# Cross attention with hard memory picks and a routed FFN: transposed projection, row-tiled heads, a router folded into the output projection, and routing per group

## The chip, the core and the metric

The kernel runs on one core of one Trainium2 chip. The metric is the device time of one execution in microseconds; three runs of the kernel before took 468.86, 470.2 and 472.27 us. All engines of the core have instruction streams of their own: PE (TensorE), DVE (VectorE), ACT (ScalarE), POOL (GpSimd) and SP (SyncE, which only issues DMAs here). They meet at semaphores, and every stream works in the order in which it is written.

## What is computed

The input `x` is (2, 1024, 256), that is 16 tiles of 128 tokens; the context has 77 rows per batch.

```python
def _L0_xattn_ref(q, kv, Wq, Wkv, Wc):
    qp = jnp.einsum('bld,ed->ble', q, Wq)
    scores = jnp.einsum('bld,bmd->blm', qp, kv)
    idx = jnp.argmax(scores, axis=-1)                     # one of 77 context rows per token
    mem = jnp.take_along_axis(kv, idx[..., None], axis=1)
    mkv = jnp.einsum('bld,ed->ble', mem, Wkv)
    mk, mv = jnp.split(mkv, 2, axis=-1)                   # 16 wide, shared by the 16 heads
    qh = qp.reshape(b, l, h, dh).transpose(0, 2, 1, 3)
    logits = jnp.einsum('bhld,bmd->bhlm', qh, mk) * scale
    attn = jax.nn.softmax(logits, axis=-1)
    out = jnp.einsum('bhlm,bmd->bhld', attn, mv)
    return jnp.einsum('bld,ed->ble', out, Wc)             # after merging the heads

x = x + xattn(layernorm(x), ctx, Wq, Wkv, Wc)
# FFN: 8 experts, 2 per token, gate = silu; hidden 256, inner 512, twice
x = x + ffn(layernorm(x), w1, w2, router_w)
```

The memory rows of a batch are copies of at most 77 different rows, so both kernels attend over the 77 context rows, each weighted by how often it was picked, and leave out those that were never picked.

## The kernel before

The program has four parts. **The head** (lines 328 to 337 on SP) loads `x`, the small weights and 12 MB of expert weights (`raw`, 8 DMAs), normalises the tokens of one batch after the other, takes the scores against the 77 rows (L943), picks the largest (`picks`) and counts the picks (`counts`, `masks`). **The attention** then goes over NH = 4 groups of 512 tokens. In a loop over u from -1 to 4, each with 10 slots, the queries of group u+1 are prepared while group u is attended and group u-1 is finished. To prepare is: normalise again (`normalise`, L678), transpose (`prep_x`, L965), project (`prep_project`, L972), lay each head out in 64 columns as high part, low part, a one and the high part again (`qs`, L509 and L684), transpose those (`prep_turn`, L985), and multiply with the keys `bd` to have the maxima (`prep_logits`, L998, `maxima`, L693). To attend is: per pair of heads two products of 77 x 512 with the keys and two that subtract the maxima (`logits`, L1017 and L1019, into the banks 0 and 1), the exponential (`exps`, L488), and per four heads the sums with the values in four column tiles of the array (`sums`, L1032), which are turned back (L1039) and divided (L777, L779). To finish (`post`) is: transpose (L1045), output projection (L1064), residual (L703), the second layernorm (L707 to L719, `pow` on POOL in L428), transpose again (L1045), router product (L1078), and the top two experts by maxima and comparisons on DVE (L737 to L761).

Beside this ACT splits the expert weights: `high(n)` (L477 to L481) writes chunk n of 48, rounded, into `W`, which overlies `raw` two chunks off; POOL subtracts it from the raw chunk (L411) into one of two buffers `low`; and `high(n + 2)` on ACT waits for that, issues its DMA to DRAM (`lows`, L477) and overwrites the raw chunk.

**The routing** comes once all groups are done (L1119 to L1130, L841 to L879): counts per expert, the slot of each token, one-hot tables, a list `idx` of rows per block. SP brings the low parts back (`W1lo` in L362 once the attention has used `qT`, `W2lo` in L369 over `X` once the last layernorm has read it) and the last rows (L351) behind them. **The FFN loop** (L1141 to L1178) works off 39 blocks of 128 rows, each gathered by an indirect DMA (L448), and starts when index, low parts and rows are there. The change does not touch it.

## Time and profile before

| | |
|---|---|
| runs | 468.86, 470.2, 472.27 us (median 470.2) |
| span of the profiled execution | 468.0 us; its own time is not among the runs, the median is 2.2 us above its span |
| PE busy | 376.7 us (80%) |
| DVE busy | 221.9 us (47%) |
| ACT busy | 197.3 us (42%) |
| POOL busy | 171.6 us (37%) |
| head, then groups 0, 1, 2 | to 67.8, 106.5, 145.8 and 184 us |
| group 3, finish of group 3, routing | to 208, 230 and 251.3 us |
| FFN loop | 251.3 to 468 us |

The ends of the groups are the starts of the first L1017 of each group; the others are read from the timeline. The span runs from the first to the last instruction. A busy share is an average over these parts, so each part is read for itself. In the rows, an arrow `<-` behind idle time names what ended it, and the granted TensorE clock is given as a share of 2.4 GHz.

### The profile page before, as it was taken

How to read it: one execution, taken by the hardware profiler on the slowest of the kernel's cores; microseconds unless marked ns; L12 is line 12 of the kernel's file. 1: busy time of each engine (PE TensorE's matmuls, PEld its weight loads, DVE VectorE, ACT ScalarE, POOL GpSimd, SP SyncE). 2: the span in 40 equal slices, each digit the busy share in tenths (PEclk: the TensorE clock that was granted, in tenths of full speed). 3: DMA queues.
4: the chain of work that ended last, by engine and by line, in shares of the span. 5: the costliest groups of instructions: out<-in, count | busy, mean ns of one | idle time of the engine just before them, and what ended most of it. 6: DMA issues, size and time to landing. Idle time of an engine off the chain costs nothing.

```text
span 468.0 us, 7576 instructions
## 1 busy us (share of the span) xinstructions
PE 376.7 (80%) x2262; PEld 282.8 (60%) x2263; DVE 221.9 (47%) x535; ACT 197.3 (42%) x376; POOL 171.6 (37%) x148
## 2 busy tenths in 40 slices
PE   1758688879999988765514999999999999999980
PEld 1647565558677655343513677777777777677760
DVE  4576734545674764543382344344344344343430
ACT  0324546666657664420101444444444444344330
POOL 2021633433333353320003245545545545544521
PEclk9967979999979998876555999999999999999986
DMA  8999110111212112229611032332332332332320
GB/s 266 386 387 336 57 34 34 46 45 35 69 45 82 68 57 87 73 91 349 223 48 46 8 62 47 57 57 46 55 59 46 51 63 46 47 67 46 50 32 11
DMA packets 35317, 43.44 MB, mean 93 GB/s; under 512 B 3200, under 2 KB 27904, under 8 KB 35296
## 3 DMA queue, kind: packets, MB, share of 16 engines
q1 hardware_dynamic: 20896, 26.49, 16.5%
q0 software_dynamic: 7488, 10.39, 13.6%
q10 hardware_dynamic: 6912, 6.29, 4.0%
q8 instruction: 12, 0.20, 0.2%
q14 instruction: 9, 0.07, 0.0%
HBM read 27.23 MB, written 15.93 MB: 92 GB/s over the span
## 4 chain that ended last, share of the span: by engine, by line
PE 74%; DVE 12%; ACT 4%; issue 4%; DMA 2%; POOL 1%; SPq 1%; DVEq 0%; POOLq 0%; ACTq 0%
PE ps L1155 24%; PE ps L1166 12%; PE ps L1173 4%; PE ps L985 4%; PE ps L972 4%; PE ps L1064 3%; PE ps L998 3%; PE ps L1017 3%; PE ps L1019 3%; PE ps L1032 3%; PE ps L1045 2%; PE ps L1141 2%; PE ps L1078 2%; ACT qs L509 1%; PE ps L943 1%
## 5 line engine op out<-in xcount | busy, mean ns | idle before, releaser
L445 POOL DMA_INDIRECT out_x<-oT,idx x39 | 61.8, 1586 | 98.8 <-ACT oT L558 98.8
L411 POOL TENSOR_TENSOR low<-raw,W 128x512 bf16 (+1 forms) x48 | 62.0, 1295 | 95.4 <-DMA lows<-low 79.6
L1155 PE MATMUL ps<-W,qs 128*128 x312 | 83.6, 411 | 1.2 <-DVE qs L884 1.2
L1155 PEld LDWEIGHTS ps<-W,qs 128*128 128x128 f32 x312 | 57.4, 191 | 13.2 <-issue 1.6
L890 DVE TENSOR_TENSOR uT<-uT,ps 128x512 f32<-128x512 f32 x39 | 26.8, 687 | 69.9 <-ACT uT L564 69.9
L564 ACT ACTIVATE uT<-ps 128x512 f32<-128x512 f32 x39 | 23.4, 599 | 85.9 <-PE ps L1155 85.9
L448 POOL DMA_INDIRECT xr<-rows,idx x39 | 38.7, 991 | 38.5 <-DVE idx L874 26.9
L894 DVE TENSOR_TENSOR qs<-ps,mT 128x512 fp32r<-128x512 f32 x39 | 27.0, 692 | 49.3 <-ACT mT L570 49.3
L1155 PE MATMUL ps<-W1lo,xpT 128*128 x156 | 41.3, 388 | 0.0
L693 DVE TENSOR_REDUCE mx<-ps 128x8 f32<-128x616 f32 x32 | 25.5, 798 | 32.7 <-PE ps L998 32.6
L488 ACT ACTIVATE pT<-ps 77x1024 f32<-77x1024 f32 x32 | 32.7, 1022 | 13.7 <-PE ps L1019 13.7
L985 PE MATMUL ps<-ident,qs 128*128 128x128 f32 x128 | 21.9, 297 | 13.5 <-DVE qs L684 8.8
L1166 PE MATMUL ps<-W,mT 128*128 x156 | 28.7, 307 | 2.0 <-DVE xpT L895 2.0
L481 ACT CAST W<-raw 128x512 fp32r<-128x512 f32 x48 | 29.8, 621 | 0.2
L1017 PE MATMUL ps<-qT,bd 128*77 128x512 f32 x64 | 29.3, 458 | 0.5 <-ACT pT L488 0.3
L558 ACT ACTIVATE oT<-ps,xr 128x256 f32<-128x256 f32 x39 | 18.5, 474 | 24.2 <-PE ps L1166 23.3
L1173 PE MATMUL ps<-ident,uT 128*128 128x128 f32 x156 | 24.3, 278 | 5.0 <-issue 3.9
L985 PEld LDWEIGHTS ps<-ident,qs 128*128 128x128 f32 x128 | 15.5, 151 | 19.6 <-DVE qs L684 16.8
L1019 PE MATMUL ps<-mT,neg 128*77 128x512 f32 x64 | 26.1, 408 | 0.0
L1166 PE MATMUL ps<-W,qs 128*128 x156 | 25.3, 285 | 0.0
L998 PEld LDWEIGHTS ps<-bd,qT 128*128 128x128 f32 x128 | 19.9, 203 | 8.6 <-issue 4.2
L494 ACT CAST qT<-ps 128x512 fp32r<-128x512 f32 x32 | 18.8, 587 | 14.4 <-PE ps L985 14.3
(171 smaller groups left out, 641.9 us busy)
## 6 DMA issues: line engine op xcount, KB each, us to landing
raw<-in_w SPq DMA_DIRECT2D x8, 1536.0 KB, 17.0
lows<-low ACTq DMA_DIRECT2D x48, 128.0 KB, 1.7
W1lo<-lows SPq DMA_DIRECT2D x8, 512.0 KB, 7.7
rows<-xr SPq DMA_DIRECT2D x4, 528.0 KB, 3.3
X<-in_x SPq DMA_DIRECT2D x2, 1024.0 KB, 6.9
out_x<-X SPq DMA_DIRECT2D x4, 512.0 KB, 3.3
X<-lows SPq DMA_DIRECT2D x8, 256.0 KB, 4.4
xr<-rows,idx POOLq DMA_INDIRECT x39, 2.8
```

Source lines behind the costliest of these rows:

```text
L411: pool.tensor_tensor(low[:, j, :], was, high.bitcast(F32), ALU.subtract).then_inc(low_ok, 1)
L445: pool.indirect_dma_start(out=out, out_offset=at_rows(c), in_=ob[:, c % GR, :], in_offset=None, compute_op=ALU.add).then_inc(sc_out, 16)
L448: pool.indirect_dma_start(out=xg[:, b % GR, :], out_offset=None, in_=rows, in_offset=at_rows(b)).then_inc(g_in[b % GR], 16)
L481: act.copy(W[:, n, :], raw[:, n + 2, :]).then_inc(hi_ok, 1)
L488: act.activation(pT[0:NK, 2 * (n % 4):2 * (n % 4) + 2, :], ps[0:NK, 0:2, :], ACT.Exp).then_inc(ex_ok, 1)
L985: mm = pe.transpose(ps[:, 5, n * P:(n + 1) * P], qs[:, a:a + 2, :].rearrange("p h w -> p (h w)"), ident[:])
L998: mm = pe.matmul(ps[:, 6 + n // 2, (n % 2) * 2 * NK:(n % 2 + 1) * 2 * NK], qT[:, w % 2, 4 * g + n, t * P:(t + 1) * P], bd[:, w // 2, :], s ...
L1017: pe.matmul(ps[0:NK, o, :], bd[:, u // 2, o * NK:(o + 1) * NK], qT[:, u % 2, p, :], start=True, stop=False)
L1019: mm = pe.matmul(ps[0:NK, o, :], neg[:, 2 * p + o:2 * p + o + 1].broadcast_to([P, NK]), mT[:], start=False, stop=True)
L1155: mm = pe.matmul(ps[:, f, :], part[:, c * P:(c + 1) * P], chunk(wts, e * per + (2 * c + f)), start=(k == 0 and c == 0), stop=(k == 2 and c ...
L1166: mm = pe.matmul(ps[:, 4, 0:D], part[:, c * P:(c + 1) * P], w2, start=(k == 0 and c == 0), stop=(k == 2 and c == FC - 1))
L1173: mm = pe.transpose(ps[:, 3, c * P:(c + 1) * P], yb[:, c * P:(c + 1) * P], ident[:])
```

## The change

- **Head.** `x` comes in four DMAs. The small weights are issued by ACT. POOL normalises (one `tensor_scalar` per tile, behind its `pow`). The 8 router columns, with the mean taken out, stand beside the 77 score columns in `GT`, so one product of 85 columns gives scores and the router's share of `x`. DVE picks with `max` and `max_index`.
- **Transposed projection.** `project` multiplies the weights, as the stationary operand, with the transposed tokens, 512 at a time, so the queries arrive transposed: `qh` and `ql`, high and low part, for all four groups before the attention starts. `prep_turn`, its copies and the second layernorm of the queries go.
- **Row-tiled heads.** `logits` multiplies in two row tiles of 64 rows, 308 columns each, three times (high with high, low with high, high with low), per tile and half of the heads. `scores_turned` takes four heads at a time: 16 products of 32 rows and 512 columns in four row tiles, into the banks 0 to 3. One exponential covers 2048 columns. `uT` is copied by ACT instead of DVE.
- **Router in the output projection.** `WC` gets 8 columns more, the product of output projection and router (once, L1103). The second transpose and the router product go; `residual` works per tile of 128 tokens and adds the share of `x`; the top two come from `max` and `max_index`.
- **Routing per group.** `ranks`, `places` and `table` work off group v beside the attention of group v+2; at the end the last two groups' share, the totals and one product that selects the blocks remain.
- **Low parts.** SP issues their DMAs, in one stream with the raw weights, the residuals and the rows; the number of `high` calls per slot stands in a table.

```diff
+STEPS = 4
+SLOTS = 2 * STEPS
+COUNTS = (6, 5)
+HIGH_HEAD = (0, 2, 3, 3)
+HIGH_SLOT = (2, 1, 1, 1, 2, 1, 1, 1)
+HIGH_FIRST = sum(HIGH_HEAD)
+def high_before(u, k):
+    n = HIGH_FIRST + u * sum(HIGH_SLOT) + sum(HIGH_SLOT[:k])
+    return min(NC, n)
...
+            def keep_lows(start, stop):
+                for n in range(start, stop):
+                    sp.wait_ge(low_ok, n + 1)
+                    sp.dma_start(lows[n], low[:, n % LR, :]).then_inc(low_out[n % LR], 16)
...
+            kept = 0
+            for v in range(NH - 1):
+                at = high_before(v + 1, SLOTS - 1)
+                keep_lows(kept, at)
                 keep_residual(v)
+                kept = high_before(v + 2, 2)
+                keep_lows(at, kept)
                 keep_rows(v)
...
+            for u in range(NH):
+                here = slice(u * HT, (u + 1) * HT)
+                pool.wait_ge(ln_v, u + 1)
+                pool.tensor_tensor(rs[:, here], ve[:, here], half[:], ALU.pow).then_inc(ln_r, 1)
+                pool.wait_ge(ln_r, u + 1)
+                for i in range(HT):
+                    q = u * HT + i
+                    if u:
+                        pool.wait_ge(x_tr, 2 * (u - 1) + i // 2 + 1)
+                    pool.tensor_scalar(xn[:, i, :], X[:, q, :], mv[:, q, 0:1], rs[:, q:q + 1],
+                                       ALU.subtract, ALU.mult).then_inc(xn_ok, 1)
...
-            def high(n):
-                if 2 <= n < NC + 2:
-                    act.wait_ge(low_ok, n - 1)
-                    act.dma_start(lows[n - 2], low[:, n % 2, :]).then_inc(low_out[n % 2], 16)
-                if n < NC:
...
+            def high(count):
+                for _ in range(count):
+                    n = highs[0]
+                    if n >= NC:
+                        return
+                    highs[0] += 1
+                    if n >= 2:
+                        act.wait_ge(low_ok, n - 1)
                     if n % EC == 0:
                         act.wait_ge(raw_in[n // EC], 16)
                     act.copy(W[:, n, :], raw[:, n + 2, :]).then_inc(hi_ok, 1)
...
+                q_high(u, 0)
+                q_high(u, 1)
+                high(HIGH_HEAD[u])
...
+            def residual(v, i):
+                q = v * HT + i
+                dve.wait_ge(wc_mm, q + 1)
+                dve.tensor_tensor(X[:, q, :], X[:, q, :], ps[:, 5, 0:D], ALU.add).then_inc(x2_ok, 1)
+                dve.tensor_tensor(g2[:, i, :], ps[:, 5, D:RW], x0[:, q, :], ALU.add).then_inc(g2_ok, 1)
+                dve.wait_ge(x2_ok, q + 1)
+                dve.bn_stats(st2[:, i, :], X[:, q, :]).then_inc(st2_ok, 1)
+                dve.wait_ge(g2_ok, q + 1)
+                dve.max(v8[:, i, :], g2[:, i, :]).then_inc(top, 1)
+                dve.wait_ge(st2_ok, q + 1)
+                dve.bn_aggr(mv2[:, i, :], st2[:, i, :]).then_inc(mv2_ok, 1)
+                dve.wait_ge(top, TOPS * v + 2 * i + 1)
+                dve.max_index(j8[:, i, :], v8[:, i, :], g2[:, i, :]).then_inc(top, 1)
...
+            def choose(v):
+                dve.wait_ge(mv2_ok, (v + 1) * HT)
+                dve.tensor_scalar(rs2[:], mv2[:, :, 1], EPS, None, ALU.add).then_inc(v2_ok, 1)
+                dve.wait_ge(top, TOPS * v + 2 * HT)
+                dve.tensor_copy(ef[:], j8[:, :, 0:2].rearrange("p t k -> p k t")).then_inc(top, 1)
+                dve.wait_ge(top, TOPS * v + 2 * HT + 1)
+                dve.tensor_tensor(o12[:].rearrange("p k t e -> p (k t) e"),
+                                  iota_f[:, 0:E].unsqueeze(1).broadcast_to([P, 2 * HT, E]),
+                                  ef[:].rearrange("p k t -> p (k t)").unsqueeze(2).broadcast_to([P, 2 * HT, E]),
+                                  ALU.is_equal).then_inc(top, 1)
...
+                dve.wait_ge(pre_mm, v + 1)
+                rank = ps[:, 5, 320:320 + HT * E].rearrange("p (t e) -> p t e", e=E)
+                for k in range(2):
+                    dve.tensor_tensor(pr[:, k], o12[:, k], rank, ALU.mult).then_inc(sl_ok, 1)
+                dve.wait_ge(sl_ok, 2 * v + 2)
+                link(dve.tensor_reduce(slot[:], pr[:].rearrange("p k t e -> p (k t) e"), AX.X, ALU.add))
+                link(dve.tensor_copy(sloti[:], slot[:]))
+                link(dve.tensor_scalar(rmi[:], sloti[:], P - 1, None, ALU.bitwise_and))
...
+                for n in range(2 * HT):
+                    i = n % HT
+                    dve.tensor_scalar(bval[:, n, :], iota_h[:], colf[:, n:n + 1], tok_f[:, v * HT + i:v * HT + i + 1],
+                                      ALU.is_equal, ALU.mult).then_inc(hot_ok, 1)
+                    dve.tensor_scalar(asel[:, n, :], iota_h[:], rmf[:, n:n + 1], None, ALU.is_equal).then_inc(hot_ok, 1)
...
-                for n in range(4):
-                    a = 2 * (4 * g + n)
-                    mm = pe.transpose(ps[:, 5, n * P:(n + 1) * P], qs[:, a:a + 2, :].rearrange("p h w -> p (h w)"),
-                                      ident[:])
-                mm.then_inc(q_tr, 1)
...
-                for n in range(4):
-                    mm = pe.matmul(ps[:, 6 + n // 2, (n % 2) * 2 * NK:(n % 2 + 1) * 2 * NK],
-                                   qT[:, w % 2, 4 * g + n, t * P:(t + 1) * P], bd[:, w // 2, :], start=True, stop=True)
-                mm.then_inc(l1_mm, 1)
...
-                for o in range(2):
-                    pe.matmul(ps[0:NK, o, :], bd[:, u // 2, o * NK:(o + 1) * NK], qT[:, u % 2, p, :],
-                              start=True, stop=False)
-                    mm = pe.matmul(ps[0:NK, o, :], neg[:, 2 * p + o:2 * p + o + 1].broadcast_to([P, NK]), mT[:],
-                                   start=False, stop=True)
-                mm.then_inc(l2_mm, 1)
...
-                if k == 5:
-                    pe.wait_ge(xn2_ok, (v + 1) * HT)
-                    turn(xn2, 0, x2_tr)
-                if k == 6:
-                    pe.wait_ge(x2T_ok, 2 * v + 1)
-                    turn(xn2, 1, x2_tr)
-                if k == 7:
-                    pe.wait_ge(x2T_ok, 2 * v + 2)
-                    for i in range(HT):
-                        for c in range(DC):
-                            mm = pe.matmul(ps[:, 3, i * E:(i + 1) * E], oT[:, i, c, :], RT[:, c, :],
-                                           start=(c == 0), stop=(c == DC - 1))
-                    mm.then_inc(r_mm, 1)
...
+            def project(u, j):
+                if u == 0:
+                    pe.wait_ge(wqt_in, 16)
+                else:
+                    pe.wait_ge(ql_ok, 2 * (u - 1) + j + 1)
+                for c in range(DC):
+                    mm = pe.matmul(ps[:, 4 + j, :], WQT[:, c, j * P:(j + 1) * P], xT[:, u % 2, c, :],
+                                   start=(c == 0), stop=(c == DC - 1))
+                mm.then_inc(q_mm, 1)
...
+                    pe.wait_ge(mx_ok, u * SLOTS + k)
+                for n, (part, hl) in enumerate(((qh, 0), (ql, 0), (qh, 1))):
+                    for r in range(2):
+                        half_ = slice(r * 64, (r + 1) * 64)
+                        mm = pe.matmul(ps[:, 6 + r, 0:HT * NK], part[half_, u, j, t * P:(t + 1) * P],
+                                       kb[half_, u // 2, hl].rearrange("p h n -> p (h n)"), start=(n == 0), stop=(n == 2))
+                mm.then_inc(l1_mm, 1)
...
+                    pe.wait_ge(xT_ok, 2 * NH)
+                    pe.wait_ge(sc_used, NH)
+                else:
+                    pe.wait_ge(ex_ok, n)
+                for m, (part, hl) in enumerate(((qh, 0), (ql, 0), (qh, 1), (None, 0))):
+                    for r in range(4):
+                        quad = slice(r * 32, (r + 1) * 32)
+                        if part is not None:
+                            keys, rhs = kb[quad, u // 2, hl, (2 * r + o) % 4, :], part[quad, u, j, :]
+                        else:
+                            h = j * 8 + 2 * r + o
+                            keys, rhs = sel[quad, h:h + 1].broadcast_to([32, NK]), mT[quad, :]
+                        mm = pe.matmul(ps[0:NK, r, :], keys, rhs, start=(m == 0), stop=(m == 3))
+                mm.then_inc(l2_mm, 1)
...
+                if i:
+                    pe.wait_ge(x2_ok, v * HT + i)
+                    pe.wait_ge(g2_ok, v * HT + i)
+                for c in range(DC):
+                    mm = pe.matmul(ps[:, 5, 0:RW], oT[:, i, c, :], WC[:, c, :], start=(c == 0), stop=(c == DC - 1))
+                mm.then_inc(wc_mm, 1)
...
+            for u in range(NH + 1):
+                for k in range(SLOTS):
+                    if u < NH and k % 2 == 0:
+                        scores_turned(u, k // 2)
+                    if u + 1 < NH:
+                        logits(u + 1, k)
+                    if u < NH and k % 2 == 1:
+                        sums(u, k // 2)
+                    if u >= 1 and k in (1, 2):
+                        turn_heads(u - 1, k - 1)
+                    if u < NH and k % 2 == 0 and k:
+                        turn_sums(u, k // 2 - 1)
+                    if u >= 1 and k == 0:
+                        turn_sums(u - 1, STEPS - 1)
+                    if u == 0 and k == 2:
+                        counts(1)
+                    if u >= 1 and 3 <= k <= 6:
+                        combine(u - 1, k - 3)
+                    if u >= 2 and k == 0:
+                        ranks(u - 2)
+                    if u >= 2 and k == 7:
+                        place(u - 2)
+                if u + 1 < NH:
```

**The order on SP.** The SP queue before, between the raw weights and the group loop:

```order
L335 DMA X<-in_x 128x8x256
L337 DMA raw<-in_w 128x6x512 x8
L341 DMA rows<-xr 128x264
L342 DMA out_x<-xr 128x256
L354 UNCONDITIONAL_BRANCH
```

and in the change, where the 48 DMAs of `low` stand in this queue:

```order
L303 DMA X<-in_x 128x4x256 x4
L306 DMA raw<-in_w 128x6x512 x8
L310 DMA rows<-xr 128x264
L311 DMA out_x<-xr 128x256
L316 DMA lows<-low 128x512 x27
L320 DMA out_x<-X 128x4x256
L316 DMA lows<-low 128x512 x4
L325 DMA rows<-xr 128x4x264
```

The low parts were issued by ACT before; now they are behind the raw weights and the two padding rows (L310, L311), and between them SP waits for a group's residual and rows.

**The order on ACT in the head of the change** (`pT` here is `xT`, `qhl` the high parts of the queries, `W` the rounded weights):

```order
L457 CAST W<-raw 128x512 [waits raw_in0]
L457 CAST W<-raw 128x512
L462 COPY pT<-ps 128x2x2x128 [waits x_tr] x2
L467 CAST qhl<-ps 128x512 [waits q_mm] x2
L457 CAST W<-raw 128x512 [waits low_ok] x3
L462 COPY pT<-ps 128x2x2x128 [waits x_tr] x2
L467 CAST qhl<-ps 128x512 [waits q_mm] x2
L457 CAST W<-raw 128x512 [waits low_ok]
```

Three casts of weights (chunks 2, 3 and 4) stand between the queries of the third and the fourth group.

**The order on PE in the attention.** Before, one slot of 10 of a group:

```order
L985 MATMUL ps<-ident,qs 128x128 [waits qT_ok,q_lo]
L985 MATMUL ps<-ident,qs 128x128 x3
L1017 MATMUL ps<-qT,bd 77x512 [waits ex_ok]
L1019 MATMUL ps<-mT,neg 77x512
L1017 MATMUL ps<-qT,bd 77x512
L1019 MATMUL ps<-mT,neg 77x512
L998 MATMUL ps<-bd,qT 128x154 [waits mx_ok,qT_ok]
L998 MATMUL ps<-bd,qT 128x154 x3
```

and in the change two slots of 8 of a group (L1013 is `scores_turned`, L974 `logits`, L1032 `turn_sums`, L1059 `combine`, L1024 `sums`):

```order
L1013 MATMUL ps<-qhl,kb 77x512 [waits ex_ok]
L1013 MATMUL ps<-qhl,kb 77x512 x11
L1013 MATMUL ps<-mT,sel 77x512 x4
L974 MATMUL ps<-kb,qhl 128x308 [waits mx_ok,ql_ok]
L974 MATMUL ps<-kb,qhl 128x308 x5
L1032 MATMUL ps<-ident,uT 128x128 [waits ut_ok]
L1032 MATMUL ps<-ident,uT 128x128 x3
L1059 MATMUL ps<-WC,oT 128x264 [waits g2_ok,x2_ok,oT_ok]
L1059 MATMUL ps<-WC,oT 128x264
L974 MATMUL ps<-kb,qhl 128x308 [waits mx_ok,ql_ok]
L974 MATMUL ps<-kb,qhl 128x308 x5
L1024 MATMUL ps<-pT,vc 32x512 [waits on_ok,ex_ok]
```

The transposes and the projection are out of the group; a product of four heads takes the place of two products of two heads.

## Rows read from the trace of the kernel before

**Rows 1.** Busy time per stretch: start:end, length, then engines, clock, DMA.

```profile
0.00:67.80 67.80, 42.48 (x257) 36.47 (x259) 40.02 (x125) 22.87 (x44) 18.35 (x28) 0.85 0.72 253
67.80:106.50 38.70, 31.90 (x204) 22.28 (x203) 17.22 (x32) 26.33 (x43) 14.81 (x12) 1.00 0.12 39
106.50:145.80 39.30, 36.43 (x229) 28.05 (x228) 24.86 (x62) 24.83 (x43) 14.44 (x12) 0.91 0.18 62
145.80:184.00 38.20, 32.81 (x201) 22.81 (x200) 22.55 (x55) 23.13 (x37) 15.03 (x12) 0.96 0.21 70
184.00:208.00 24.00, 18.16 (x102) 11.34 (x100) 14.31 (x44) 8.97 (x13) 7.42 (x7) 0.86 0.17 56
208.00:230.00 22.00, 14.43 (x44) 10.68 (x44) 4.89 (x16) 1.82 (x4) 1.01 (x1) 0.58 0.93 295
230.00:251.30 21.30, 3.32 (x64) 2.77 (x64) 16.33 (x47) 0.23 (x1) 2.46 (x3) 0.50 0.22 73
251.30:468.00 216.70, 197.15 (x1170) 148.35 (x1170) 81.72 (x156) 89.08 (x196) 98.03 (x76) 0.96 0.29 48
```

**Rows 2.** DMA issues: queue, count, KB each, us from issue to landing.

```profile
lows<-low ACTq DMA_DIRECT2D x48, 128.0 KB, 1.7
X<-lows SPq DMA_DIRECT2D x8, 256.0 KB, 4.4
rows<-xr SPq DMA_DIRECT2D x1, 132.0 KB, 12.4
```

**Rows 3.** SP's issues in the head: start, length, instruction.

```profile
5.66 26.52 SPq L337 DMA_DIRECT2D raw<-in_w  x8
32.77 1.94 SPq L341 DMA_DIRECT2D rows<-xr  x1
```

**Rows 4.** PE's timeline around the first products of group 1.

```profile
106.82 0.60 PE L985 MATMUL ps<-ident,qs 128*128 128x128 f32 x4
107.18 0.47 PE L1017 MATMUL ps<-qT,bd 128*77 128x512 f32 x1
...
108.19 0.57 PE L998 MATMUL ps<-bd,qT 128*128 128x154 f32 x4
108.69 1.07 PE L1032 MATMUL ps<-pT,vc 77*32 77x512 f32 x8
...
110.65 1.89 PE L1064 MATMUL ps<-WC,oT 128*128 128x256 f32 x8
```

**Rows 5.** Groups of instructions: count, busy us, mean ns, idle before.

```profile
L488 ACT ACTIVATE pT<-ps 77x1024 f32<-77x1024 f32 x32 | 32.7, 1022 | 13.7 <-PE ps L1019 13.7
L693 DVE TENSOR_REDUCE mx<-ps 128x8 f32<-128x616 f32 x32 | 25.5, 798 | 32.7 <-PE ps L998 32.6
L719 DVE TENSOR_SCALAR xr<-X,mv,rs 128x256 f32<-128x256 f32 x16 | 7.4, 524 | 1.5 <-POOL rs L428 1.5
L707 DVE BATCH_NORM_STATS2 st<-X 128x6 f32<-128x256 f32 x16 | 6.0, 418 | 0.3
```

**Rows 6.** The timeline of POOL and DVE while both work in SBUF.

```profile
172.78 2.51 POOL L411 TENSOR_TENSOR low<-raw,W 128x512 bf16 x2 [0.90 <-DMA lows<-low]
...
173.01 1.10 DVE L744 TENSOR_TENSOR o<-eq,f 128x32 f32<-128x32 f32 x1
```

**Rows 7.** The chain that ended last: start, us, what; finish of group 3.

```profile
209.91 3.79 PE ps L1064 x8
...
226.36 3.59 PE ps L1078 x16
```

**Rows 8.** The timeline from the last layernorm to the first gather.

```profile
224.94 3.54 SPq L369 DMA_DIRECT2D X<-lows  x7
...
242.04 4.63 DVE L867 TENSOR_TENSOR pT<-iota_h,rmh 128x1024 f16<-128x1024 f16 x4
...
248.23 1.19 POOL L448 DMA_INDIRECT xr<-rows,idx  x1 [26.92 <-DVE idx L874]
...
251.35 0.66 PE L1141 MATMUL ps<-ident,xr 128*128 128x128 f32 x2 [4.17 <-DMA xr<-rows,idx]
```

1242 lines of the change are left out of this document (595 added, 647 removed).

## The prediction

> **What bounds the kernel now.** I read the busy time per stretch first, then the timelines of single engines in the stretch that a term is about, then the chain that ended last and the DMA table. The reader is to see four stretches with four limits. The FFN loop takes 216.7 us with PE busy for 197.15 of them [rows 1]; its text is unchanged, so I carry it over as it is. Groups 0 to 2 take 38.7, 39.3 and 38.2 us with PE busy for 31.9, 36.4 and 32.8: PE bounds them. The finish of group 3 (22.0 us) runs at a clock of 0.58 with no engine busy for long; it is a chain of handovers. The routing (21.3 us) is DVE alone, 16.33 us busy, and ends at the gather at 248.23 and the first transpose at 251.35 [rows 8]. So what counts is when the FFN loop starts: at 251.3 now.
>
> **The head.** It ends at 67.8 with PE at 42.5 of 67.8 us [rows 1]. Of the change's head I add up PE: per group 8 transposes (0.36 per four at full clock [rows 4]; 0.7), 8 products of 85 columns (estimate 1.8, at most one weight load each), and four of 512 columns in full precision: L1064's 8 passes of 256 columns cover 1.89 us, some 0.16 of it the end of the last [rows 4], so 8 passes of 512 cost 3.5. That is 6 us per group at full clock; DVE has about as much (picks, moments, two subtractions). With some 13 us of setup the third group would be through at about 35. There the queue order decides. The low parts now stand on SP behind 12 MB of raw weights. The padding row issued at 32.77 landed 12.4 us later, at 45.2 [rows 2, 3], while a low part on ACT's queue took 1.7 (median). Cast 4 waits for low part 2, and that for the buffer which low part 0 frees on landing: with one more padding row and 0.25 MB more to load, at about 47.5. The Trainium skill, "DMA: Bandwidth & Descriptors", section on queues, rings and completion order, says that a DMA engine consumes the descriptors of one ring in their order; the 12.4 us agree. Then subtraction 1.3, cast 0.6, and group 3's copies, which stand behind it on ACT: 50. Scores, projections and subtractions of group 3 take 7 us more; then four `logits`, each waiting for the maxima before it (0.75 + 0.8 [rows 5]), the turned maxima and their copy: group 0 starts at about 65.5, only 2.3 us earlier. Without the wait it would be some 10 us earlier still.
>
> **Groups 0 to 3.** One `scores_turned`: 16 products of 512 columns. Before, four such take 1.01 us (107.18 to 108.19 [rows 4]). If the four row tiles run side by side, the four rounds take 1.01; if one after the other, 4.04. No row tile is in this trace; the nearest row is L1032, where four column tiles, eight passes of 512 columns in full precision, take 1.07 us, while by L1064 (1.73 / 8 for 256 columns) they would cost 8 x 0.43 = 3.5 in turn. I take 1.3, near the lower end, because 16 weight loads come with it, and keep 4.0 for a rival. One `logits`: six products of 308 columns; L998 has four of 154 columns in 0.50, its weight load as long as its columns. Side by side 0.64, in turn 0.9; I take 0.75. Two stood per tile before too, and their transposes (L985), the projection and the second normalisation leave the group.
>
> PE per full group: 4 x 1.3 + 8 x 0.75 + sums 4 x 1.07 + 16 transposes 1.7 + maxima 0.4 + output projection 16 x 0.22 = 3.6 + ranks and table 1.6, together 22.8. DVE: maxima 8 x 0.8 = 6.4, divisions 2.8, residual and router about 1.4 per tile (0.42 for the statistics [rows 5], the add the same, four small ones near 0.17) = 5.6, `choose` 1.3, `scaled` 1.9 (4 x 0.41 and two small), `weighed` 0.8, `places` about 4.0 (16 compares of 128 columns: L867 has 1024 columns in 1.22 [rows 5, 8], so 0.15 to 0.2), table 0.3: 23. ACT: 4 x 1.87 (L488's 1.02 plus 0.85 for 1024 more columns), 10 casts 6.2, 6 to 7 copies 4: 18. So PE and DVE are level, and where both are full their order costs: at a group's start DVE has 6.5 us before PE gets its next `logits`. And DVE meets POOL: L744, 128 x 32, took 1.10 instead of about 0.19, and ended while POOL's subtraction was ending [rows 6]. The change has more such small operations and as many subtractions; I put 3 us on group 2 and 2 on group 3.
>
> - Group 0 has no finish and no routing: exponential, sums and products in turn, 4 x 4.8 + 2, plus masks of batch 1: 23.
> - Group 1, finish but no routing: 25.
> - Group 2, everything: 27 + 3 = 30.
> - Group 3, no `logits` for a next one: 19 + 2 = 21.
>
> 65.5 + 99 = 164.5, against 208.
>
> **Finish of group 3.** DVE: last division 0.8, `places` 4.0, `scaled` 1.9, `weighed` 0.8, then the residual chain and `choose`: 7. With the turn ahead 15.2. The output projection of 8 passes took 3.79 at the low clock against 1.73 [rows 7, 4], so per tile 0.95 more, of which about 3 us show. The router product (3.59 [rows 7]) and two transposes are gone. To 182.7, so 18 instead of 22.
>
> **Routing.** Ranks 0.9, `places` 4.0, `scaled` 1.9: the last layernorm is done at 189.5. From here two chains run. The index: table, weights, totals and the last selection, some 6 us, 195.5. The low parts of w2 need `X` free: eight issues (seven take 3.54 [rows 8]), 4.4 to land [rows 2], 198, and the rows of group 3 behind them, 528 KB, 199.5. The second is later, where before the index was. Plus 3.1 from gather to transpose (248.23 to 251.35): **the FFN loop starts at 202.5** instead of 251.3, 49 us earlier. A FFN loop alike gives 468.0 - 49 = 419 for the span; the median of the runs is 2.2 above the span, so **421 us**.
>
> **Rivals.**
> 1. *Mode changes cost.* PE now goes from four row tiles to two, to none, to column tiles, six times per pair of slots, 24 per group. Before, a column-tiled step stands between untiled ones, and L1032 with both changes takes 1.07 for 0.85 of columns, so 0.1 per change at most there; it is in my prices. An upper end is the pipeline behind one product of 512 columns, L1017's 0.47 minus its 0.25 spacing, 0.22: 96 changes less what I have counted, +22 us: 443. Chance 0.13. The Trainium skill, "TensorEngine Tiling (Array Packing)", key properties, says that changing the mode drains the engine and speaks so against this change; no row here has a change between two row tilings.
> 2. *The row tiles do not overlap.* 16 x (4.04 - 1.3) = +44, `logits` +5, some of it under DVE's excess: 461, and then the change does not do what it says. Against it: column tiles overlap [rows 4]. Chance 0.07. The same skill in "TensorE: Matmul & The Clock Gate", part 3, reports 3.07 times for four row tiles; by that page a `scores_turned` would be an estimated 4.04 / 3.07 = 1.32, and the sum stays.
> 3. *Slower than before: the row tiles do not overlap and PE falls to the low clock in the groups.* Then one `scores_turned` costs 8 us, +107 us, 520. The clock was 0.91 to 1.00 in groups 0 to 2 and 0.58 where PE was busy two thirds [rows 1]; dense products would keep it up. It decides from 4.4 us per `scores_turned` on (1.3 + 49/16). Chance 0.04.
> 4. *The head has no stall and DVE's overlap is free.* -10 in the head, -5 in the groups, -4 in the finish: 402. Chance 0.08.
>
> **How the numbers follow.** The forecast, 421, has 0.68; its own range is 405 to 440 (prices of PE 1.0 to 1.6 per `scores_turned`, +-5; order costs on DVE +-7; finish and routing +-5). The range 399 to 447 takes in rivals 1 and 4; outside are 2, 3 and a tail, 0.17. A measurement of this kernel tells 1% (4.7 us) from no change. Faster by over 1%: 0.93 (forecast, 1, 4 and most of 2); within 1%: 0.02; slower: 0.05.
>
> **What would show it.** Right: ACT idle near 36 to 48 before its third cast of group 2 of the head, ended by a subtraction that waited for a low part; 16 products of `scores_turned` within 1.2 to 1.5 us; groups near 25 us with PE and DVE both above 75%; the last `rows` DMA, not the index, ahead of the first gather; an FFN loop of 216 to 218 us. Wrong: spacings of 0.25 us between the row tiles' products; a gap at each change of tiling; POOL or ACT as the engine that others wait for in the groups, because the low parts on SP stand behind a residual that comes late; or an FFN loop that moved although it is unchanged.

## The result, and the profile after

The changed kernel takes **447.39 us** (median of 4 runs, 444.47 to 449.63) against 471.24 (4 runs, 468.86 to 474.59): ratio **0.9513** [0.9434, 0.9593], 24 us less. Forecast were 421 us and a range of 399 to 447: the side was right, half of the forecast gain did not come, and the time lies 0.4 us outside the range.

The busy time per stretch of the changed kernel, cut at the same events as before (columns as there), answers to [rows 1]. The profiled execution took 444.47 us, the fastest of the four; its span is 442.6 us.

```profile
0.00:71.10 71.10, 47.10 (x228) 33.76 (x229) 37.78 (x162) 16.16 (x31) 35.58 (x43) 0.82 0.69 243
71.10:99.14 28.04, 24.32 (x177) 12.45 (x178) 13.60 (x31) 15.53 (x19) 12.15 (x10) 0.67 0.13 44
99.14:122.70 23.56, 21.55 (x188) 11.95 (x188) 14.69 (x51) 16.60 (x21) 13.18 (x12) 1.00 0.19 64
122.70:153.90 31.20, 23.95 (x201) 13.96 (x201) 23.36 (x86) 16.72 (x22) 14.75 (x12) 0.89 0.26 88
153.90:182.60 28.70, 21.76 (x153) 10.65 (x153) 18.59 (x74) 16.26 (x21) 11.90 (x10) 0.76 0.18 61
182.60:203.80 21.20, 11.45 (x38) 6.81 (x37) 13.70 (x75) 1.29 (x3) 2.69 (x3) 0.57 0.69 223
203.80:226.30 22.50, 1.52 (x15) 1.11 (x15) 11.43 (x52) 0.23 (x1) 2.54 (x4) 0.50 0.59 184
226.30:442.60 216.30, 194.35 (x1150) 147.16 (x1170) 81.76 (x156) 88.96 (x196) 98.04 (x76) 0.97 0.30 48
```

| stretch | forecast | measured | off by |
|---|---|---|---|
| head | 65.5 | 71.1 | +5.6 |
| group 0 | 23 | 28.0 | +5.0 |
| group 1 | 25 | 23.6 | -1.4 |
| group 2 | 30 | 31.2 | +1.2 |
| group 3 | 21 | 28.7 | +7.7 |
| finish of group 3 | 18 | 21.2 | +3.2 |
| routing | 19.8 | 22.5 | +2.7 |
| FFN loop | 216.7 | 216.3 | -0.4 |

Group 1 stands at a granted clock of 1.00 with PE busy 91%, and came out shorter than forecast. The head, group 0, group 3 and the finish stand at 0.82, 0.67, 0.76 and 0.57, and these four carry 21.5 of the 23.6 us that are missing. In four other profiles with the same work in the groups (e2, e3, e4 and e8 below) group 0 took 28.0 to 32.3 us and group 2 31.3 to 34.3, so the 28.0 and 31.2 of this execution are at the low end.

Group 0 has no long wait of PE in this execution. Its clock had fallen before, at the end of the head, where PE waits about 1 us before one `logits` after the other (each line has start, length, instruction, and the idle time before it with its releaser):

```profile
65.31 0.69 PE L974 MATMUL ps<-kb,qhl 64*128 64x308 f32 x6 [0.98 <-DVE mx L648]
66.98 1.14 PE L974 MATMUL ps<-kb,qhl 64*128 64x308 f32 x6 [0.98 <-DVE mx L648]
```

It stayed at half (0.50, that is 1.2 of 2.4 GHz) until about 91 us. Here is where the clock falls in group 2: the timeline of PE first.

```profile
127.68 0.93 PE L1013 MATMUL ps<-qhl,kb 32*77 32x512 f32 x12
128.44 0.41 PE L1013 MATMUL ps<-mT,sel 32*77 32x512 f32 x4
133.60 1.14 PE L974 MATMUL ps<-kb,qhl 64*128 64x308 f32 x6 [4.75 <-DVE mx L648]
134.67 1.11 PE L1046 MATMUL ps<-ident,xn 128*128 128x128 f32 x4
```

VectorE's timeline at the same time, in `places`:

```profile
126.43 1.24 DVE L748 CAST sloti<-slot 128x8 int32<-128x8 f32 x1
127.70 1.22 DVE L749 TENSOR_SCALAR rmi<-sloti 128x8 int32<-128x8 int32 x1
...
132.66 0.80 DVE L648 TENSOR_REDUCE mx<-ps 128x8 f32<-128x616 f32 x1
```

POOL's, two subtractions of 1.26 us each:

```profile
126.37 2.53 POOL L391 TENSOR_TENSOR low<-raw,W 128x512 bf16<-128x512 f32 x2 [2.60 <-ACT W L457]
```

And ACT's:

```profile
135.10 0.23 ACT L493 ACTIVATE ex<-lm 128x32 f32<-128x32 f32 x1 [6.72 <-DVE lm L718]
...
135.75 1.87 ACT L478 ACTIVATE pT<-ps 77x2048 f32<-77x2048 f32 x1
```

VectorE makes `places` in one piece, 125.9 to 132.66, before it takes the maxima (`mx`) that PE's next `logits` waits for. PE stands 4.75 us, and then works at half clock: `logits` takes 1.14 there and 0.69 elsewhere, four transposes 1.11 and not 0.66. ACT meanwhile waits 6.72 us for `lm` (the router's values, the end of VectorE's `scaled`), with the next exponential queued behind that wait. In group 3 the same burst holds PE for 4.99 us through ACT; the sums behind it take 1.93 us and not 1.07:

```profile
167.94 1.93 PE L1024 MATMUL ps<-pT,vc 77*32 77x512 f32 x8 [4.99 <-ACT pT L478]
```

The finish and the start of the FFN loop answer to [rows 7, 8]. On PE's timeline, the output projections 2.78 us apart at half clock and the loop's first transpose:

```profile
193.78 2.10 PE L1059 MATMUL ps<-WC,oT 128*128 128x264 f32 x4 [0.68 <-DVE g L675]
196.56 2.10 PE L1059 MATMUL ps<-WC,oT 128*128 128x264 f32 x4 [0.68 <-DVE g L675]
...
226.48 0.66 PE L1164 MATMUL ps<-ident,xr 128*128 128x128 f32 x2 [10.32 <-DMA xr<-rows,idx]
```

On SP's, the issue of w2's low parts and of group 3's rows:

```profile
210.65 3.94 SPq L349 DMA_DIRECT2D X<-lows  x8
214.64 0.49 SPq L325 DMA_DIRECT2D rows<-xr  x1
```

And on POOL's the first gather, which those rows' landing releases:

```profile
223.23 1.23 POOL L421 DMA_INDIRECT xr<-rows,idx  x1 [19.36 <-DMA rows<-xr]
```

The last layernorm was done 6.85 us into the routing (203.8 to 210.65; 6.8 were forecast). From there to the gather it took 12.6 us where the forecast has 10.0 (189.5 to 199.5). So what the routing took too long lies in SP's issues and their landing, not in the clock.

### The profile page after: what moved, and what is told of

Read it like the earlier page. It is cut to its first block, busy times and chain, and to the rows that moved or that the text cites. A ratio compares the mean times of both kernels' runs of the same rounds, so it can differ in the third digit from the quotient of the medians.

```text
span 442.6 us, 7229 instructions
## 1 busy us (share of the span) xinstructions
PE 346.0 (78%) x2148; PEld 237.9 (54%) x2169; DVE 214.9 (49%) x684; ACT 171.8 (39%) x314; POOL 190.8 (43%) x165
## 4 chain that ended last, share of the span: by engine, by line
PE 65%; DVE 15%; DMA 6%; POOL 5%; issue 4%; ACT 2%; SPq 1%; ACTq 0%; POOLq 0%; DVEq 0%
PE ps L1178 25%; PE ps L1189 12%; PE ps L1059 5%; PE ps L974 4%; PE ps L1196 4%; PE ps L1013 4%; POOL xn L382 3%; PE ps L1024 2%; DVE mx L648 2%; PE ps L1164 2%; DMA rows<-xr 2%; PE ps L935 2%; DVE oh L758 2%; DMA WKV<-in_WkvT 2%; PE ps L1032 1%
## 5 line engine op out<-in xcount | busy, mean ns | idle before, releaser
L391 POOL TENSOR_TENSOR low<-raw,W 128x512 bf16<-128x512 f32 x48 | 60.8, 1276 | 76.6 <-ACT W L457 70.0
L1178 PE MATMUL ps<-W,kb 128*128 x312 | 84.5, 413 | 1.2 <-DVE kb L866 1.2
L1178 PEld LDWEIGHTS ps<-W,kb 128*128 128x128 f32 x312 | 57.4, 191 | 13.8 <-issue 1.6
L876 DVE TENSOR_TENSOR kb<-ps,mT 128x512 fp32r<-128x512 f32 x39 | 27.0, 692 | 48.7 <-ACT mT L547 48.7
L974 PE MATMUL ps<-kb,qhl 64*128 64x308 f32 x192 | 26.6, 389 | 14.9 <-DVE mx L648 14.9
L1178 PE MATMUL ps<-W1lo,oh 128*128 x136 | 36.5, 384 | 1.5 <-issue 0.2
L478 ACT ACTIVATE pT<-ps 77x2048 f32<-77x2048 f32 x16 | 30.0, 1874 | 14.8 <-PE ps L1013 14.8
L974 PEld LDWEIGHTS ps<-kb,qhl 64*128 64x128 f32 x192 | 17.6, 225 | 26.0 <-issue 19.6
L1059 PE MATMUL ps<-WC,oT 128*128 128x264 f32 x64 | 22.7, 487 | 6.3 <-ACT oT L489 4.3
L1024 PE MATMUL ps<-pT,vc 77*32 77x512 f32 x128 | 20.5, 718 | 7.0 <-ACT pT L478 6.8
L1189 PE MATMUL ps<-W,kb 128*128 x156 | 24.6, 280 | 0.0
L547 ACT CAST mT<-ps 128x512 fp32r<-128x512 f32 x39 | 22.6, 581 | 4.8 <-PE ps L1196 4.8
L1189 PE MATMUL ps<-X,oh 128*128 x156 | 23.8, 275 | 0.0
```

The lines of the kernel that those rows point to most:

```text
L391: pool.tensor_tensor(low[:, n % LR, :], raw[:, n + 2, :], W[:, n, :].bitcast(F32), ALU.subtract).then_inc(low_ok, 1)
L478: act.activation(pT[0:NK, 4 * (n % 2):4 * (n % 2) + 4, :], ps[0:NK, 0:4, :], ACT.Exp).then_inc(ex_ok, 1)
L974: mm = pe.matmul(ps[:, 6 + r, 0:HT * NK], part[half_, u, j, t * P:(t + 1) * P], kb[half_, u // 2, hl].rearrange("p h n -> p (h n)"), start ...
L1024: mm = pe.matmul(ps[r * 32:(r + 1) * 32, 4, :], vc[:, u // 2, :], pT[0:NK, 4 * (n % 2) + r, :], start=True, stop=True)
L1059: mm = pe.matmul(ps[:, 5, 0:RW], oT[:, i, c, :], WC[:, c, :], start=(c == 0), stop=(c == DC - 1))
L1178: mm = pe.matmul(ps[:, f, :], part[:, c * P:(c + 1) * P], chunk(wts, e * per + (2 * c + f)), start=(k == 0 and c == 0), stop=(k == 2 and c ...
```

## Experiments

Single executions of the changed kernel lie between 444.5 and 453.5 us, so each row gives its ratio to the kernel before, run on the same chip, with its interval. e5 is the changed kernel once more, run with e6 to e8:

> The changed kernel itself, once more, beside the next three, since its own executions lie 1% apart and the kernel before stood 0.5% higher in the last comparison. Expected: 0.951 of the kernel before, some 448 to 450 us, and in the profiled execution groups whose lengths differ from the first profile only where the granted clock does.

| run | edit | us | ratio |
|---|---|---|---|
| changed kernel | | 447.39 | 0.9513 [0.9434, 0.9593] |
| e5 | none | 450.40 | 0.9500 [0.9418, 0.9582] |
| e1 | `weights` late | 453.12 | 0.9589 [0.9536, 0.9643] |
| e2 | products tile by tile | 450.60 | 0.9504 [0.9435, 0.9573] |
| e3 | cast 4 behind group 3's copies | 446.61 | 0.9466 [0.9404, 0.9528] |
| e4 | rows before places at the end | 450.40 | 0.9530 [0.9484, 0.9577] |
| e6 | compares of `places` spread | 445.69 | 0.9447 [0.9394, 0.9500] |
| e7 | `masks(1)` spread | 446.98 | 0.9433 [0.9354, 0.9511] |
| e8 | normalisation on VectorE | 450.56 | 0.9541 [0.9488, 0.9594] |
| e9 | e1 and e6 | 449.20 | 0.9539 [0.9468, 0.9610] |
| e10 | head's order | 440.84 | 0.9385 [0.9307, 0.9463] |
| e11 | e1, e4, e6, e7, e10 | 444.11 | 0.9445 [0.9380, 0.9510] |
| e12 | all products on one row tile | 544.03 | one run |
| e13 | fillers in the groups | 446.85 | 0.9456 [0.9383, 0.9529] |
| e14 | e6, e7, e10 | 439.48 | 0.9284 [0.9210, 0.9358] |
| e15 | e14 with fillers | 427.19 | 0.9029 [0.8959, 0.9099] |
| e16 | POOL's subtraction narrow | 441.40 | 0.9310 [0.9242, 0.9379] |
| e17 | e15, fillers to the end | 422.47 | 0.8996 [0.8923, 0.9070] |
| e18 | e17 and e1 | 425.39 | 0.9076 [0.9020, 0.9133] |

**First theory: ACT stands behind a wait.** e1:

```diff
-                    if u >= 2 and k == 1:
+                    if u >= 2 and k == 4:
                         weights(u - 2)
-                        if k == 2:
+                        if k == 4:
                             weighed(v)
-                kept = high_before(v + 2, 2)
+                kept = high_before(v + 2, 4)
```

> Edit: ACT computes a group's router exponential behind slot 4's exponential of the next group but one, not in slot 1; VectorE's use of it moves to slot 4 too; SP keeps the low parts of slots 2 and 3 ahead of the rows. Theory A (the in-order ACT queue stood behind a wait for `lm`, the end of VectorE's `scaled`): in the trace of the changed kernel ACT idled 6.72 us (group 2) and 4.55 us (group 3) there, with `pT` exponentials queued behind; so 8 to 12 us less than the changed kernel's 447, that is 435 to 439, and no idle time of ACT that ends at VectorE's `lm`. Rival B (VectorE's own queue, `places` stretched by POOL, is the bound of groups 2 and 3, and ACT only waited beside it): the groups keep their lengths of 31.2 and 28.7 us, total within 2 us of 447, and PE's waits for `mx` grow by what its waits for `pT` lose. Rival C (the delay only moves to the next event in the ring, the low parts behind the rows on SP): the ACT waits come back as waits for low parts, total 443 to 447.

ACT's wait was gone, and group 2 became longer: 35.8 us, where profiles with that part unchanged have 31.2 to 34.3. PE's timeline of e1 in group 2:

```profile
134.61 1.14 PE L974 MATMUL ps<-kb,qhl 64*128 64x308 f32 x6 [5.67 <-DVE mx L648]
...
138.65 1.93 PE L1024 MATMUL ps<-pT,vc 77*32 77x512 f32 x8
```

And ACT's, its exponentials of slots 2 and 4:

```profile
128.99 1.87 ACT L478 ACTIVATE pT<-ps 77x2048 f32<-77x2048 f32 x1
...
144.62 1.88 ACT L478 ACTIVATE pT<-ps 77x2048 f32<-77x2048 f32 x1 [2.87 <-PE ps L1013]
```

The exponential ran 6.8 us earlier (128.99 for 135.75), PE stood 5.67 us for `mx` all the same, and the sums took 1.93 us at half clock. Theory A falls as far as the wait alone is concerned; B is right that VectorE's burst comes first, but its "within 2 us" was missed as well (453.12 us; by the ratios 0.8% more than the changed kernel, inside the intervals).

**Do row tiles work side by side?** e2 swaps two loops of `scores_turned`; e12 instead reads every operand from partitions 0 to 31 and so leaves out three quarters of the heads; it is a measurement only.

```diff
-                for m, (part, hl) in enumerate(...):
-                    for r in range(4):
+                for r in range(4):
+                    for m, (part, hl) in enumerate(...):
```

```diff
-                        quad = slice(r * 32, (r + 1) * 32)
+                        quad = slice(0, 32)
```

> Edit: `scores_turned` issues its 16 products row tile by row tile (four in a row on one tile), not turn by turn over the four tiles; same products, same sums. Theory A (products on different row tiles run beside each other, which is what makes a group's 16 scores cost 1.1 us at full clock): four in a row on one tile do not overlap, except where one tile's last and the next one's first meet; 16 x 0.25 us or more each, about 4 us in place of 1.1 for each of 16 calls, some +46 us on PE's queue, of which 35 to 45 us show: 480 to 495. Rival B (order does not matter, since a tile's products are pulled apart by the accumulation into one bank anyway): within 2 us of 447. Rival C (PE is not the bound of a group, about 23 us of chain through ACT and VectorE is): about +2.9 us a call are partly hidden, 455 to 470.

> Edit: `scores_turned` takes the operands of all 16 products from partitions 0 to 31, so that all go to one row tile; they still write four banks. It leaves out three quarters of the heads (a measurement only). With products issued tile by tile the 16 took as long as turn by turn, 1.1 us, which left open whether row tiles work beside each other at all. Theory A (they do, and the order does not matter since a tile's products queue up by themselves): on one tile the 16 can only follow each other, 3.4 us or more at full clock, 6.8 at half. Rival B (a product of 32 rows is simply short, whatever tile it is on): 1.1 us as before.

PE's timeline of e2, at full clock:

```profile
113.80 0.95 PE L1013 MATMUL ps<-qhl,kb 32*77 32x512 f32 x12
114.55 0.43 PE L1013 MATMUL ps<-mT,sel 32*77 32x512 f32 x4
```

And that of e12, first at half and then at full clock:

```profile
150.81 5.40 PE L1013 MATMUL ps<-qhl,kb 32*77 32x512 f32 x12
156.01 1.90 PE L1013 MATMUL ps<-mT,sel 32*77 32x512 f32 x4
...
164.71 3.00 PE L1013 MATMUL ps<-qhl,kb 32*77 32x512 f32 x12
167.55 1.09 PE L1013 MATMUL ps<-mT,sel 32*77 32x512 f32 x4
```

16 products over four row tiles take 1.2 us tile by tile (113.80 to 114.98), 1.1 to 1.2 turn by turn; on one tile 3.9 us at full clock (164.71 to 168.64) and 7.1 at half. So the tiles do work side by side, whatever the order of issue, and rivals 1 and 2 of the prediction are out. My expectation for e2 was wrong: the order does not matter. What the overlap is worth is 2.8 us per call at full clock, 45 us for 16 calls (an estimate from these rows). The whole of e12, one execution, is some 97 us longer, since its clock was 0.56 in the groups (76 to 326 us).

**The head.** e3 and e8 each take away one thing on which group 3's copies or the turns of the tokens might wait.

```diff
-HIGH_HEAD = (0, 2, 3, 3)
+HIGH_HEAD = (0, 2, 2, 4)
```

```diff
-                    pool.tensor_scalar(xn[:, i, :], X[:, q, :], mv[:, q, 0:1], rs[:, q:q + 1],
+                    dve.tensor_scalar(xn[:, i, :], X[:, q, :], mv[:, q, 0:1], rs[:, q:q + 1],
```

> Edit: of the eight copies of weights that ACT makes in the head, two and not three stand ahead of group 3's copies, four and not three behind. Theory A (ACT stood in the head behind copy 4, which waits for a low part, which POOL makes only behind its last normalisations and which SP's queue then takes 4 us to land; in the trace of the changed kernel copy 4 came at 49.21 us and group 3's copies from 49.73): group 3's copies start 5 to 6 us earlier, the head's last products and VectorE's maxima with them; 5 to 7 us less than 447, that is 440 to 442, since the clock then also falls less. Rival B (POOL's normalisations at 1.25 us each set when group 3 can be turned at all): 1 to 3 us less. Rival C (what the head gives, ACT's fourth copy behind group 3 takes back, at the turned maxima): within 1 us of 447.

> Edit: the head's 16 normalisations of x leave POOL (1.25 us each in the trace of the changed kernel) for VectorE (the same form took 0.35 us there in `scaled`); POOL keeps the power of -0.5. Theory A (the head waits on POOL, twice: for x at the turns, and for the first low parts, which POOL makes only behind its 16 normalisations, and on which ACT's copy 4 ahead of group 3's copies waits): the first turn some 3 us earlier, group 3's copies 3 to 6 us earlier, 3 to 6 us less in all. Rival B (VectorE is the head's bound, 37.8 us busy of 71, and gets 5.6 us more): 0 to 5 us more. Moving cast 4 alone gave 0.8 us at the first exponential (72.35 for 73.15).

In e3 group 3's copies began at 46.51, 3.2 us earlier, and the first exponential at 72.35 and not 73.15: PE still stood 3.24 us for `mx`, behind `masks(0)` and `picks(2)`, and went on at half clock. So the stop for copy 4 was real, but hardly anything hung on it alone: the prediction's "without the wait it would be some 10 us earlier still" is not borne out. e8 changed nothing: with POOL free at 36.7, the second pair of its subtractions still had to wait for low part 0 to land. SP's timeline of e8:

```profile
38.21 14.20 SPq L316 DMA_DIRECT2D lows<-low  x5
```

POOL's, two pairs of subtractions:

```profile
36.72 2.49 POOL L385 TENSOR_TENSOR low<-raw,W 128x512 bf16<-128x512 f32 x2
47.69 2.50 POOL L385 TENSOR_TENSOR low<-raw,W 128x512 bf16<-128x512 f32 x2 [8.48 <-DMA lows<-low]
```

And ACT's copy 4:

```profile
48.99 0.62 ACT L451 CAST W<-raw 128x512 fp32r<-128x512 f32 x1 [5.16 <-POOL low L385]
```

The part was issued at about 38.2, right behind the raw weights, and landed at 47.7. That is the prediction's step for the head, and it held: 47.5 was forecast, copies at 50, measured 49.73. What was not forecast is what stands beside it, VectorE's masks and picks, and what comes behind it. e10 moves the six copies behind the group (HIGH_HEAD 0, 2, 0, 6) and PE's and VectorE's `logits` 1 to 3 behind the projection:

```diff
-                if u == NH - 1:
-                    logits(0, 1)
                 score(u, (0, 1))
-                if u == NH - 1:
-                    logits(0, 2)
                 score(u, (2, 3))
-                if u == NH - 1:
-                    logits(0, 3)
                 project(u, 0)
                 project(u, 1)
-            for k in range(4, SLOTS):
+            for k in range(1, SLOTS):
                 logits(0, k)
```

> Edit: in the head's last group all six copies of weights stand behind ACT's own work for the group (HIGH_HEAD 0, 2, 0, 6), TensorE makes the group's scores and projection before `logits` 1 to 3 of group 0, and VectorE takes their maxima behind its picks. Theory A (TensorE stood 3.6 and 2.2 us there, for `mx` behind `masks` and `picks` and for ACT behind copy 4, and everything up to slot 2 of group 0 then ran at half clock): no pause over 1.5 us before the projection, which takes 3.63 us in place of 5.07, first exponential at 66 to 69 us in place of 73.15; group 0 begins at a higher clock and takes 24 to 27 us in place of 27 to 32; in all 7 to 11 us less than the changed kernel. Rival B (with the copies moved behind the group the low parts fall behind, and ACT or SP pays for it in groups 0 and 1): first exponential earlier, but only 2 to 4 us less in all. Rival C (the half clock of group 0 is not due to the head's pauses): first exponential 2 to 3 us earlier and no more.

PE's timeline of e10, at the end of the head and in group 0:

```profile
46.15 3.70 PE L945 MATMUL ps<-pT,WQT 128*128 128x512 f32 x8 [0.44 <-DVE qhl L608]
...
86.57 1.14 PE L973 MATMUL ps<-kb,qhl 64*128 64x308 f32 x6 [5.54 <-DVE mx L648]
```

The projection is back at 3.70 us and the first exponential at 67.75, as A expected. In group 0, though, `masks(1)` stopped PE for 5.54 us, with half clock behind. That is not the edit's doing: e2, with the head of the changed kernel, has the same wait.

```profile
92.24 1.14 PE L974 MATMUL ps<-kb,qhl 64*128 64x308 f32 x6 [5.57 <-DVE mx L648]
```

In these two executions PE was back at full clock at 77 and 83 us, and reached the `logits` in question long before `masks(1)` was through; in the profile of the changed kernel it was at half clock until about 91 us and had nothing to wait for there. Group 0 took 31.4 and 32.3 us against 28.0. In all e10 is 1.3% below the changed kernel, and the intervals overlap.

**Bursts spread.** e6 takes `places`' 16 compares out of slot 0, e7 cuts `masks(1)` into four pieces, e9 joins e1 and e6, e14 joins e6, e7 and e10, and e11 all edits with e4.

```diff
+PAIRS = (0, 0, 1, 2, 4, 4, 6, 7, 8)
+                    if u >= 2:
+                        pairs(u - 2, PAIRS[k], PAIRS[k + 1])
-                    if u == 0 and k == 3:
-                        masks(1)
+                    if u == 0 and k >= 3:
+                        next(later, None)
```

> Edit: the 16 compares of `places` (8 pairs of `bval` and `asel`, 0.39 us a pair) leave slot 0 and are spread over slots 1 to 7; nothing else moves. Theory A (a burst on VectorE withholds `mx` from TensorE, which then stands 5 us and works at half clock for some 10 us behind that; in the late-weights run the wait of ACT was gone and group 2 was longer all the same, 36.7 us, with TensorE idle 5.67 us for `mx`): the pause shrinks from 5.7 to about 2.6 us in groups 2 and 3 and less is done at half clock; 6 to 12 us less than the changed kernel in the same comparison. Rival B (POOL's subtractions hold the short operations in `places`' head, four of about 1.2 us in place of 0.17, and they stay in slot 0): 2 to 4 us less, groups 2 and 3 still with a pause over 3.5 us. Rival C (the work of VectorE in all, not its place, sets the group): within 1.5 us.

> Edit: VectorE's `masks(1)` (17 short chained operations and two of 1.5 us, 7.2 us in all) leaves slot 3 of group 0 and is spread over slots 3 to 6, where VectorE has room. Theory A (the burst makes TensorE stand about 4 us in group 0 and keeps the clock low; group 0 took 28 to 31 us in four profiles of kernels that are equal up to there, at clocks of 0.67 down to 0.51): group 0 takes 23 to 26 us, 3 to 5 us less in all. Rival B (the clock is low in group 0 since the head ended with a pause, and rises only by itself): within 1.5 us of the changed kernel in the same comparison.

> Edit: both of the earlier ones at once, the compares of `places` spread over slots 1 to 7 and the router's exponential behind slot 4's. Alone, the late exponential gave a longer group 2 (36.7 us) and the spread compares about 0.6% of the whole. Theory A (two queues block one after the other, ACT behind `lm` and VectorE in `places`; taking one away only lets TensorE run into the other, and each such pause costs a stretch at half clock): the two together are worth more than their sum, groups 2 and 3 come to 24 to 27 us each, 8 to 12 us less than the changed kernel, 438 to 442. Rival B (their effects add): 447 to 451. Rival C (a pause of about 3 us remains in slot 0, from POOL's collisions in the integer conversions, and that alone keeps the clock at half): 444 to 447.

> Edit: the head's order, `masks` of group 0 spread, compares spread, late router exponential, and the rows before the places behind the last group, all together. Theory A (pauses of TensorE and the half clock behind them are what kept the change from its 49 us): 422 to 432 us, mean granted clock before the FFN loop over 0.85, with the largest pause of TensorE between 50 and 180 us under 3 us. Rival B (the whole of the work on VectorE, about 20 us a group with POOL's collisions, is the next bound and close): 434 to 440. Rival C (edits only move the pauses): over 442.

> Edit: the head's order (the best alone, about 1.3% below the changed kernel), `masks` of group 0 spread and the compares of `places` spread; the router's exponential and the order behind the last group stay as in the changed kernel. Theory A (each took a pause from a different group, and the late exponential was what cost in the run of all edits): 434 to 439. Rival B (VectorE's total in groups 2 and 3 is the bound, so that spreading gives nothing there): 439 to 442, groups 2 and 3 each over 28 us.

e6: PE's pause in group 2 fell to 1.69 us, the stretch behind it was at half clock still, and 0.6% less is inside the intervals. e7 is inconclusive alone. e9 was not worth more than its parts. e14 gave 2.4% less than the changed kernel, outside the intervals, e11 0.7% less: with e1 and e4 in it the same edits are worth less. For e11 theories A and B were missed; over 442 us is what rival C had, that edits only move the pauses.

**Rows first at the end.** e4:

```diff
             v = NH - 1
-            places(v)
             scaled(v)
-            table(v)
             weighed(v)
+            places(v)
+            table(v)
```

> Edit: behind the last group VectorE makes the rows and their weights first (`scaled`, `weighed`), and then the ranks' masks and the table. Theory A (from the last group to the FFN loop the chain is VectorE's `scaled` at 209.2 us, SP's issue of W2's low parts, 3.9 us, SP's issue of the rows, their landing at 223.1; the index had been ready at 216.9): the rows start about 4 us earlier and the index comes 3 to 4 us later and takes over as the last; 3 to 5 us less than 447, that is 442 to 444. Rival B (the transfers that run at that time set the landing, not the issue): within 1 us of 447. Rival C (the index's chain, with its many short steps on VectorE and PE, grows more than its slack of 6 us): 1 to 3 us more than 447.

From the last choice to the first transpose of the loop it took 20.6 us in place of 22.7 (210.65 to 231.27, and 203.8 to 226.48), but the total did not show it (A had 3 to 5 us less). SP still waited 3.5 us for group 3's residual to land before it could issue w2's low parts. And e4 is the changed kernel word for word up to there, and its profiled execution was 6.9 us later by then. Busy time and clock of the changed kernel from 80 us on:

```profile
80.00:88.00 8.00, 8.00 (x62) 4.54 (x58) 4.87 (x15) 3.48 (x4) 2.58 (x3) 0.50 0.10 35
88.00:96.00 8.00, 6.61 (x60) 3.90 (x56) 5.60 (x13) 6.07 (x7) 4.45 (x4) 0.88 0.16 52
```

And of e4:

```profile
88.00:96.00 8.00, 7.08 (x44) 3.29 (x40) 4.88 (x11) 4.00 (x5) 3.80 (x3) 0.50 0.15 49
```

The same instructions, within a microsecond of each other, one time at 0.88 and one time at 0.50, and 2.4 us more in group 0 alone. Such differences are part of why executions of one kernel lie 1% apart, and they pointed at the clock as a cause and not a companion. The first of the three lines says something else too: PE was busy for all of 8 us and stayed at 0.50. What brings the full clock back no run here settles.

**The clock by itself.** e13 only adds work: products into a bank that nobody reads then, where PE would stand. e15 adds such fillers to e14, e17 more of them to e15.

```diff
+            def warm(n, bank):
+                for _ in range(n):
+                    pe.matmul(ps[:, bank, 0:P], ones[:], tri[:], start=True, stop=True)
+                    if (u, k) in WARM:
+                        pe.wait_ge(ut_ok, u * STEPS + k // 2)
+                        warm(WARM[u, k], 4)
```

> Edit: only work is added to the changed kernel: TensorE makes 50 products of 128x128 bf16 into the bank of the sums, whose content is not used, in slot 4 of group 0, and 60 each in slot 2 of groups 2 and 3, at the places where it stands 4 to 5.5 us for `mx` or `pT`. Theory A (the pause itself takes the clock away): the granted clock in the 10 us behind each stays at or near 1.00 in place of 0.50 to 0.72, and groups 0, 2 and 3 are shorter by 1 to 4 us each although TensorE has more to do; 4 to 9 us less than the changed kernel. Rival B (the low clock comes with the stretch, whatever TensorE does, or is only a sign of the wait): the same lengths or longer by what the fillers overrun, 0 to 4 us more. Rival C (fillers hold the clock, but VectorE's queue is the bound of groups 2 and 3, so that TensorE at full clock only waits longer): clock up, time within 2 us.

> Edit: as the kernel before it in this comparison, with fillers besides: 12 products of 128x128 bf16 ahead of each of the head's last seven `logits`, 14 and 10 around the turned maxima, and 20 to 24 in slot 6 of group 0 and slot 2 of groups 2 and 3. Theory A: the head's tail and the start of group 0 stay at full clock; the first exponential about 3 us earlier and group 0 about 2 to 4 us shorter than in the kernel before it; 428 to 434. Rival B (as with the fillers alone: the clock does not follow the pauses): 0 to 4 us more than the kernel before it.

Busy time and clock of e14, from 50 to 80 us:

```profile
50.00:65.00 15.00, 7.31 (x44) 5.07 (x44) 7.19 (x12) 4.09 (x7) 7.50 (x6) 0.60 0.15 52
65.00:80.00 15.00, 13.33 (x107) 6.92 (x110) 4.36 (x10) 7.36 (x9) 5.05 (x4) 0.60 0.08 28
```

And of e15:

```profile
50.00:65.00 15.00, 13.34 (x170) 10.16 (x169) 7.05 (x11) 4.65 (x9) 7.55 (x6) 1.00 0.17 55
65.00:80.00 15.00, 12.93 (x152) 7.21 (x150) 10.44 (x22) 13.09 (x15) 9.22 (x8) 1.00 0.19 63
```

e15 is e14 plus 172 products that nothing needs, and is 12 us faster (427.19 for 439.48, ratios 0.9029 and 0.9284). The clock stood at 1.00 from 50 to 130 us; the first exponential came at 64.92 and not 68.61, and group 0, from first exponential to first exponential, took 21.95 us and not 27.55. The useful work of these stretches is the same, and nothing but work and waits was added, so the difference is the clock. e13, fillers alone, gave 0.6%, inside the intervals: the clock behind the 60 fillers of group 2 was 1.00 (130 to 140 us), but VectorE's burst was as long as before, and PE only waited at full clock, as its rival C had it. In the changed kernel fillers in the groups were thus not enough; on top of e14 they were worth 12 us. Whether it takes the shorter bursts is not shown: 108 of e15's fillers stand at the end of the head, where e13 has none, and fillers there without e14's edits were not tried.

**What POOL does to VectorE.** e16 leaves out most of the low parts, to make POOL's subtractions short; it is a measurement only:

```diff
-                    pool.tensor_tensor(low[:, n % LR, :], raw[:, n + 2, :], W[:, n, :].bitcast(F32), ALU.subtract
+                    pool.tensor_tensor(low[:, n % LR, 0:64], raw[:, n + 2, 0:64], W[:, n, 0:64].bitcast(F32), ALU.subtract
```

> Edit: POOL subtracts only 64 of each low part's 512 columns; it leaves out the other low parts (a measurement only). POOL's operation then takes about 0.3 us in place of 1.26. Theory A (VectorE's short operations of 0.17 us that took 1.1 to 1.25 us were held by a POOL operation; there are three or four in each of `places` and `masks`): they all take 0.15 to 0.35 us, the pauses in groups 0, 2 and 3 lose 2 to 3 us each, and with less at half clock behind them 6 to 10 us less than the changed kernel. Rival B (the long ones are the conversions to and from integers, and long by themselves): the same durations, within 1.5 us.

VectorE's timeline of e16 in `places`, in group 2 as above, to be held against the same two operations, 1.24 and 1.22 us, above:

```profile
126.40 0.28 DVE L749 CAST sloti<-slot 128x8 int32<-128x8 f32 x1
126.72 0.17 DVE L750 TENSOR_SCALAR rmi<-sloti 128x8 int32<-128x8 int32 x1
```

0.28 and 0.17 us: A holds for the durations, and the whole kernel is 2% faster (9 us by the ratios, outside the intervals). PE's waits fell from 4.75 to 2.87 us in group 2 and from 4.99 to 2.48 in group 3; where the rest of the 9 us lies is open. The Trainium skill, "SBUF — State Buffer", section "Who interferes with whom", says that VectorE and GpSimd share a port pair, and that in some modes of VectorE's the instruction that is issued first holds it for its whole length while the other engine is fully blocked. The trace agrees: POOL's subtractions start first (126.37 for 126.43), each of the two operations ends with one of them, and its 1.24 us are that subtraction's (1.26) and not its own.

**To the end.** e17 adds this to e15, and e18 adds e1's edit to that:

```diff
+                    if u == NH and 3 <= k <= 6:
+                        warm(16 if k == 3 else 9, 0)
                     if u >= 1 and 3 <= k <= 6:
                         combine(u - 1, k - 3)
                     if u >= 2 and k == 7:
+                        warm(24 if u == 2 else 12, 0)
                         place(u - 2)
```

> Edit: the fastest so far (head's order, spread, fillers) with more fillers, all into a bank of scores that is free then: 24 before `place` of group 2's slot 7, 10 and 8 around the turned maxima, 12 before each turn of the last group's heads, 16 and then 9 before each of its `combine`. Theory A (the low clock at the end of group 2, 0.59 in the profile's 140 to 150 us, and of the last group, 0.50 from 170 on, is the work of the 1.7 us and 2.1 us pauses there; a `combine` of the last group is 1.16 us and not 2.13 at full clock): group 2 takes 25 to 28 us in place of 31.3, the last group's four `combine` come 1.7 us apart and not 2.78; 8 to 11 us less, 416 to 420. Rival B (VectorE's work of about 25 us bounds group 2 at full clock as well): 3 to 6 us less.

> Edit: as the kernel before it in this comparison, with the router's exponential behind slot 4's, the edit that alone was worth nothing or 1% too much. Theory A (with TensorE's pauses filled the clock no longer pays for a moved pause, so what is left is the wait itself, 1.1 us for `pT` in each of groups 2 and 3): 1 to 3 us less than the kernel before it. Rival B (the pause moves to the place's and the table's chain in slot 7, for which nothing is filled in group 3): 0 to 3 us more.

PE's timeline of e18 in the last group's finish (e17 has the same fillers there):

```profile
172.03 1.13 PE L1076 MATMUL ps<-WC,oT 128*128 128x264 f32 x4 [0.18 <-DVE g L680]
...
173.92 1.13 PE L1076 MATMUL ps<-WC,oT 128*128 128x264 f32 x4 [0.26 <-DVE g L680]
```

A `combine` takes 1.13 us in place of 2.10 and they come 1.9 us apart in place of 2.78. e17 is the fastest version, 422.47 us, 0.8996 of the kernel before, and some 5% under the changed kernel; the 0.4% between e15 and e17 alone is inside the intervals. Its theory A was missed in group 2, which took 32.6 us and not 25 to 28 (in the profiled execution, of 426.11 us). Busy time and clock of e18 in group 2, group 3 and the finish:

```profile
109.20:139.45 30.25, 26.32 (x271) 16.46 (x271) 25.19 (x86) 16.86 (x23) 14.78 (x12) 1.00 0.29 97
139.45:165.10 25.65, 19.14 (x185) 10.78 (x185) 21.68 (x77) 16.32 (x21) 12.39 (x10) 1.00 0.22 74
165.10:180.50 15.40, 12.18 (x121) 10.46 (x121) 13.21 (x73) 1.30 (x3) 2.33 (x3) 0.89 0.40 124
```

So at full clock throughout, group 2 still takes 30 us and group 3 almost 26, with PE busy 26.32 (fillers included) and 19.14 us of it: the clock is not what bounds them there. The finish takes 15.4 us here, and 15.6 in e17, where its clock is 1.00.

e18 was not faster than e17. e1's edit stood on the slower side in four comparisons (e1, e9 beside e6, e11 beside e14, e18 beside e17, by 0.8 to 1.7%; only e11 beside e14 is clear of the intervals, and it has e4 too). The traces show where the time goes. In e18 the product that selects the blocks is 4.3 us earlier than in e17 (192.20 for 196.54), and the loop starts 1.1 us later (208.43 for 207.31). What SP waits for in e18 from 160 to 200 us, us in total, times, longest:

```profile
SPq L327 <- DVE xr L733: 8.3, 1, 8.3
SPq L351 <- DMA out_x<-X: 6.0, 1, 6.0
```

In e17 the same two waits are 3.8 and 1.0 us. With the weights made in slot 4, group 2's rows (L327) are ready later beside the rest; behind them SP issues w1's low parts, then group 3's residual, and only when that has landed w2's low parts (L351), on which the loop waits. From the ranks' last product to the loop's first transpose it is 25.6 to 27.9 us in the four runs with e1's edit, and 20.1 to 22.4 in the changed kernel and the other runs.

## Why the prediction was half right

- **FFN loop carried over:** right, 216.3 for 216.7.
- **`scores_turned` 1.3 us, `logits` 0.75:** right, 1.1 and 0.63 at full clock, and no visible cost of changing modes (group 1: 23.6 us, PE busy 21.55). All rivals that rested on PE's tiling were wrong.
- **The step that failed is the clock: the end of the head and groups 0, 2 and 3 were priced as if PE kept its full clock, with rival 3's reason that "dense products would keep it up".** Granted were 0.82, 0.67, 0.89 and 0.76. The order costs ("3 us on group 2 and 2 on group 3") have a burst on VectorE by its own length, and not PE's wait for it nor the stretch at half clock behind that wait. With the clock held up, e15 is 12 us faster than e14. The reason itself fails too: group 1 was dense and stood at 1.00, but in group 0 PE was busy 24.32 of 28.04 us at 0.67, and from 80 to 88 us all the time at 0.50. Before the falls that I read stood waits of PE, of 0.98 us in the head, 4.75 in group 2 and 4.99 in group 3; the profile of before had a warning in its finish, 0.58 with PE busy 14.43 of 22 us [rows 1].
- **Head 65.5, measured 71.1:** copies at 50 was right to 0.3 us, and the four `logits` behind the projection took the 6.2 us of the sum. The 7 us between took 13: scores (2.00 us per eight products; sixteen take 2.02 at full clock) and projection (5.07 for 3.6) ran at half clock, some 3.4 us more, and two `logits` of 1.14 that stand between them are not in the term.
- **Group 0, 28.0 for 23:** half clock from the head on. At 1.00, and with `masks(1)` spread, it is 21.9 in e15.
- **Group 3, 28.7 for 21:** only some 3 us of the 7.7 are the clock, as an estimate from e18, which takes 25.65 at 1.00. The other 4.6 are the term itself: it says 19 + 2 without a working for the 19, and VectorE alone is busy 18.59 us there (21.68 in e18).
- **Group 2, 31.2 for 30:** met, with luck in this execution, since e2, e4 and e8 took 33.4 to 34.3. At full clock e18 takes 30.25.
- **POOL's collisions** were in the same 5 us, and that was low: e16 shows 9 us for the whole kernel with what follows from them.
- **ACT's wait for `lm`** was not in the forecast. It is real (6.72 and 4.55 us) but covers the same time as VectorE's burst; taken away alone it gave nothing (e1).
- **Finish 21.2 for 18:** the sum had 15.2 us and 3 for a low clock. e17 takes 15.6 at 1.00, so the 15.2 held, and what was too small is the price of the low clock: 5.6 us by these two stretches, and not 3.
- **Routing 22.5 for 19.8:** the chain was named rightly (w2's low parts, rows, their landing, not the index); issue and landing took 12.6 us for 10.0.

The sum behind the forecast, 421, is near the 422.5 of e17, but that is partly luck: e17 is not the change alone but has the reordered head, the spread bursts and the fillers besides, its group 2 takes 32.6 us and its group 3 over 27, and its head and group 0 are shorter than forecast. The Trainium skill, "TensorE: Matmul & The Clock Gate", part 1, says that pauses between bursts of products bring the half rate back, and warns of kernels that swing between the two. The traces agree: behind 4.75 us of idle time `logits` takes 1.14 us and not 0.69. That work which nobody needs can pay for itself is shown by e15 alone.

## What to carry to other kernels

When a change takes work from the engine that bounds a stretch, the longest burst on any other engine can become its pause; price the half clock behind each pause of PE, not only the pause. Look at the granted clock stretch by stretch in the new profile before moving waits about: single edits that took a wait away gave from 0.8% more to 1.3% less, none of it clear of the intervals; spread bursts, the head's order and filled pauses together gave 5%. A test for it is cheap: add products that nothing needs where PE stands, and see if the whole gets shorter. Try them where the clock first falls: in the groups alone they gave 0.6%, inside the intervals.

## What the runs showed of the hardware

- 16 products of 32 rows and 512 columns over four row tiles take 1.1 to 1.2 us in turn and tile by tile alike; on one tile 3.9 us.
- POOL's `tensor_scalar` of 128 x 256 with two operands per partition takes 1.2 to 1.3 us (four in 4.83), VectorE's 0.35 (four in 1.37).
- Two operations of VectorE on 128 x 8 elements take 1.24 and 1.22 us beside subtractions of POOL's of 1.26 us, and 0.28 and 0.17 us beside POOL's operations of 0.32 us (e16).
- The same instructions up to there in two kernels: granted clock 0.88 and 0.50 in the same 8 us of two executions, and 2.4 us between them in that group (the changed kernel and e4). In the 8 us before, PE was busy all the time at 0.50 in both.
- A product of 128 x 128 in bf16 costs PE 0.06 us (60 in 3.52), 24 of them 1.51 us.
